# Context attentions: each product of probabilities and values in four column tiles of 32 queries in place of two of 64

## The chip, the cores and the metric

The kernel runs on one core of one Trainium2 chip. The metric is the device time of one execution in microseconds (us); for the kernel before the median of three runs is 1125.13 us (1124.1 to 1125.45). PE is the matrix engine (TensorE), PEld its weight loads, DVE, ACT and POOL are the vector, scalar and GpSimd engines, SP is the engine that issues most of the DMAs.

## The reference, cut to what matters

The reference is a four-layer chain over `x` of shape (8, 256, 256): eight samples of 256 tokens, width 256. Three of its steps are cross-attentions to a context of 77 positions per sample, with 16 heads of width 16; they differ in projections, norms and mask or bias, but all end in the same two lines (layer 0 is shown):

```python
attn = jax.nn.softmax(scores * D_QKV ** (-0.5), axis=-1)
out = jnp.einsum('bhts,bhsk->bhtk', attn, v)
```

Between and behind them stand a quantized feed-forward layer with a convolution, a self-attention with a mixture of eight experts, a routed spline layer, a pair of products with the context, and a quantized product. All of that is untouched here.

## The kernel before, in words

A context attention (`lay` 0, 1, 2) works through `NT` = 16 query tiles of `P` = 128 tokens, two for each sample; `u` is the tile. The probabilities of all 16 heads of a tile stand side by side, 16 × 77 = 1232 columns, and are cut into `NCH` = 10 chunks of 128 columns, whatever head they belong to. A chunk touches two or three heads. The values stand in `a_VB`, for each chunk a block-diagonal matrix of 128 rows and 17 columns per head touched (16 values and a column of ones, which gives the sum of the probabilities): 34 columns for five of the chunks, 51 for the other five.

For each tile the steps are, on the engines named:

- PE, `scores` (L1079): queries times keys, in four row tiles of 32 rows, 154 columns each, into PSUM banks 0 to 3.
- DVE: in layers 0 and 2 the mask or bias is added (L476) and the row maximum taken (L478), POOL subtracts it (L727); in layer 1 DVE takes the maximum (L464) and subtracts it (L467). ACT takes the exponential (L863).
- PE, `probs` (L1089): the ten chunks are transposed in three groups of 4, 4 and 2; ACT copies them from PSUM to SBUF (L868, `a_PT`) and so frees the bank.
- PE, `outputs` (L1113): for each chunk the transposed probabilities are the stationary operand and `a_VB` the moving one; the output of 128 queries is made in pieces of `OUT_COLS` queries, each in its own column tile of the array and its own partitions of PSUM bank 6 or 7. The chunks accumulate. The groups 0, 1 and 2 are three bursts, with other steps of PE between them.
- DVE: reciprocal of the sums (L485) and the product with it (L486); PE `turned` (L1120) transposes, ACT copies (L889), PE `projected` (L1126) multiplies by the output weights, DVE adds the residual (L493).

PE is fed by a program order written out by hand in `att_pe`. In the steady part of a layer it is, for tile `u`: `turned(u - 1)`, `scores(u + 2)`, `outputs(u, 0)`, `probs(u, 2)`, `outputs(u, 1)`, `projected(u - 1)`, `outputs(u, 2)`, projections and transposes for later samples (`extra`, L1003 to L1037), then `probs(u + 1, 0)` and `probs(u + 1, 1)`. `outputs` waits once per group for ACT's copy (semaphore `ring_free`), group 0 also for the residual of tile `u - 2` (`y_done`); its last product tells DVE that the tile is full (`o_full`).

All of these products are fp32. The trace holds two weight loads and two matmuls for each fp32 product of the program: 3 layers × 16 tiles × 10 chunks × 2 pieces = 960 products of L1113 stand as 1920 pairs. Where products of several tiles of the array follow each other, the pairs come in groups with one pair for every tile.

Of the kernel before, what the change touches and what calls it, by code (L numbers as in the profile page):

```python
# [123 lines left out]
def program(nc, pack0, pack1, pack2, x_in, ctx_in, ctxT_in, w1T_in, w2T_in, ew1_in, ew2_in, out):  # L124
    with ExitStack() as ctx:
# [128 lines left out]
        for c in range(NCH):  # L254
            at, done = CHUNKS[c], (CHUNKS[c - 1] + P if c else 0)
            while done < at + P:
# [1 line left out]
                end = min((h + 1) * S2, at + P)  # L258
                PIECES.append((c, h - FIRST[c], done - at, end - at, h, done - h * S2, end - h * S2))
                done = end  # L260
        QROWS, OUT_COLS = 32, 64

        KB_WORDS, VB_WORDS, V_WORDS = C * 2 * B * S2, NCH * MAXS * B * (DH + 1), H * B * (DH + 1)
        F_END = 3 * C * FF + FC * (S + 2) + FC * 3 * P
# [3337 lines left out]
```

## Time and profile before

| | |
|---|---|
| median of three runs | 1125.13 us (1124.1 to 1125.45) |
| the profiled execution's own time | 1122.43 us |
| its span, first to last instruction | 1120.7 us |
| PE busy | 1049.6 us, 94% of the span, 8906 matmuls |
| PE weight loads busy | 826.1 us, 74%, 8906 loads |
| DVE busy | 748.5 us, 67% |
| ACT busy | 469.1 us, 42% |
| POOL busy | 531.8 us, 47% |
| mean granted clock of TensorE | 0.986 |
| context attention 0 | about 33 to 137 us |
| context attention 1 | about 250 to 371 us |
| context attention 2 | about 890 to 1007 us |

A busy PE is one that has an instruction in flight; since matmuls overlap and their ends are modelled, its rate is read from the distance of starts, not from the mean duration of one. All times in the rows are microseconds from the span's start unless they are marked ns. The chain of work that ended last is followed back from an end to what released each step; a row of it gives start, length and the work, so that the lengths add up to the time.

### The profile page before, as it was taken

How to read it: one execution, taken by the hardware profiler on the slowest of the kernel's cores; microseconds unless marked ns; L12 is line 12 of the kernel's file. 1: busy time of each engine (PE TensorE's matmuls, PEld its weight loads, DVE VectorE, ACT ScalarE, POOL GpSimd, SP SyncE). 2: the span in 40 equal slices, each digit the busy share in tenths (PEclk: the TensorE clock that was granted, in tenths of full speed). 3: DMA queues.
4: the chain of work that ended last, by engine and by line, in shares of the span. 5: the costliest groups of instructions: out<-in, count | busy, mean ns of one | idle time of the engine just before them, and what ended most of it. 6: DMA issues, size and time to landing. Idle time of an engine off the chain costs nothing.

```text
span 1120.7 us, 23972 instructions
## 1 busy us (share of the span) xinstructions
PE 1049.6 (94%) x8906; PEld 826.1 (74%) x8906; DVE 748.5 (67%) x1698; ACT 469.1 (42%) x940; POOL 531.8 (47%) x526
## 2 busy tenths in 40 slices
PE   9999889988899999999989999999999999999896
PEld 5676656666676567999868999999998567765564
DVE  4899879999987448889842222222222899987794
ACT  2555677775565202121112222222222446654475
POOL 5645335577873214768764010000354757541464
PEclk9999999999999999999969999999999989999999
DMA  5999900002000300000147141311221200000001
GB/s 186 368 404 389 388 8 2 23 4 91 2 1 2 107 0 1 1 11 29 57 145 304 60 174 46 113 37 37 66 80 38 67 11 11 1 1 1 0 20 57
DMA packets 45137, 93.78 MB, mean 84 GB/s; under 512 B 3934, under 2 KB 19071, under 8 KB 42487
## 3 DMA queue, kind: packets, MB, share of 16 engines
q1 hardware_dynamic: 36646, 62.24, 15.7%
q0 software_dynamic: 7104, 29.14, 7.2%
q8 instruction: 59, 0.97, 0.3%
q10 hardware_dynamic: 1296, 1.18, 0.3%
q14 instruction: 32, 0.25, 0.1%
HBM read 39.02 MB, written 51.51 MB: 81 GB/s over the span
## 4 chain that ended last, share of the span: by engine, by line
PE 64%; DVE 19%; POOL 5%; ACT 5%; issue 4%; DMA 2%; POOLq 1%; PEldq 0%; DVEq 0%; ACTq 0%; SPq 0%; PEld 0%
PE PS L2520 11%; PE PS L2530 11%; PE PS L1113 4%; PE PS L2029 4%; PE PS L2385 3%; PE PS L1089 3%; PE PS L1126 3%; PE PS L1079 2%; PE PS L1908 2%; PE PS L2374 2%; PE PS L1743 2%; POOL big L695 2%; DVE scr L476 2%; PE PS L1037 1%; PE PS L970 1%
## 5 line engine op out<-in xcount | busy, mean ns | idle before, releaser
L2554 ACT ACTIVATE scr<-PS,W 128x128 f32<-128x128 f32 x148 | 53.5, 367 | 191.1 <-PE PS L2520 191.1
L2520 PEld LDWEIGHTS PS<-scr 128*128 128x128 f32 x992 | 116.5, 192 | 5.5 <-issue 1.8
L2520 PE MATMUL PS<-scr 128*128 128x128 f32 x992 | 118.7, 276 | 1.9 <-issue 1.5
L2530 PE MATMUL PS<-scr 128*128 128x256 f32 x496 | 112.2, 379 | 0.0
L2585 DVE TENSOR_SCALAR scr<-PS,W 128x128 f32<-128x128 f32 x148 | 51.2, 350 | 88.0 <-PE PS L2520 88.0
L727 POOL TENSOR_TENSOR scr<-scr,small 128x1232 f32<-128x1232 f32 x32 | 72.0, 2250 | 73.1 <-DVE small L478 73.0
L2591 DVE TENSOR_TENSOR scr<-PS,W 128x256 f32<-128x256 f32 x37 | 15.7, 425 | 127.0 <-PE PS L2530 123.1
L2530 PEld LDWEIGHTS PS<-scr 128*128 128x128 f32 x496 | 91.8, 190 | 11.2
L868 ACT ACTIVATE big<-PS 128x512 f32<-128x512 f32 x144 | 73.0, 523 | 58.7 <-PE PS L1089 58.1
L2631 POOL DMA_DIRECT2D expert_out<-scr x28 | 15.2, 544 | 161.4 <-DVE scr L2591 159.5
L1089 PE MATMUL PS<-W,scr 128*128 128x128 f32 x480 | 78.6, 284 | 9.4 <-ACT big L846 3.0
L1089 PEld LDWEIGHTS PS<-W,scr 128*128 128x128 f32 x480 | 52.2, 141 | 23.9 <-ACT big L846 4.6
L2385 PE MATMUL PS<-W,scr 128*128 128x128 f32 x512 | 61.1, 278 | 2.4 <-DVE scr L2140 2.4
L1113 PEld LDWEIGHTS PS<-scr,big 128*64 128x64 f32 x1280 | 45.2, 137 | 22.0 <-issue 20.5
L2385 PEld LDWEIGHTS PS<-W,scr 128*128 128x128 f32 x512 | 58.5, 192 | 3.4 <-DVE scr L2140 3.3
L863 ACT ACTIVATE scr<-scr 128x1232 f32<-128x1232 f32 x48 | 58.7, 1223 | 4.3 <-POOL scr L727 2.7
L1908 PE MATMUL PS<-identb 128*128 128x512 bf16 x225 | 58.5, 402 | 0.3 <-ACT big L868 0.3
L1113 PE MATMUL PS<-scr,big 128*64 128x34 f32 (+1 forms) x1280 | 56.7, 228 | 1.1 <-ACT big L868 0.9
L1126 PE MATMUL PS<-W,big 128*128 128x256 f32 x192 | 55.3, 410 | 0.5 <-ACT big L889 0.5
L695 POOL TENSOR_TENSOR big<-big,neghalf 128x32 f32<-128x32 f32 x8 | 45.5, 5687 | 15.9 <-DVE big L431 15.7
L1743 PE MATMUL PS<-big,W 64*64 64x256 f32 x768 | 47.0, 382 | 1.3 <-ACT scr L1662 1.3
L478 DVE TENSOR_REDUCE small<-scr 128x16 f32<-128x1232 f32 x32 | 45.9, 1436 | 1.1
(432 smaller groups left out, 2424.1 us busy)
## 6 DMA issues: line engine op xcount, KB each, us to landing
expert_in<-zeros SPq DMA_DIRECT2D x1, 19712.0 KB, 59.9
expert_out<-zeros SPq DMA_DIRECT2D x1, 19712.0 KB, 112.4
scr<-ew_in POOLq DMA_DIRECT2D x12, 1024.0 KB, 6.4
scr<-expert_in SPq DMA_DIRECT2D x38, 128.0 KB, 2.1
big<-ew_in POOLq DMA_DIRECT2D x4, 1024.0 KB, 8.5
expert_out<-scr POOLq DMA_DIRECT2D x28, 128.0 KB, 2.0
W<-pack SPq DMA_DIRECT2D x1, 2458.0 KB, 8.6
W<-pack SPq DMA_DIRECT2D x1, 2152.0 KB, 9.1
```

Of the source, the lines that this page charges most:

```text
L695: g.tensor_tensor(a_qr[j % 2], a_qvar[j % 2], neghalf[:, 0:T * H], ALU.pow).then_inc(s["qr_ready"], 1)
L727: g.tensor_tensor(sc3, sc3, a_mx[u % 3].unsqueeze(2).broadcast_to([P, H, S2]), ALU.subtract).then_inc(s["sub_ready"], 1)
L863: a.activation(a_sc[lay][u % 3], a_sc[lay][u % 3], ACT.Exp, scale=scale).then_inc(s["p_ready"], 1)
L868: a.activation(a_PT[lay][u % 2][:, 4 * g:4 * g + n, :], bank(ring_bank(lay, "p", u, g), n * P).rearrange("p (c n) -> p c n", c=n), ACT.Cop ...
L1089: ins = pe.transpose(bank(b, P, k * P), a_sc[lay][u % 3][:, at:at + P], ident)
L1113: ins = pe.matmul(PS[k:k + OUT_COLS, 6 + u % 2, at:at + n * (DH + 1)], a_PT[lay][u % 2][:, c, k:k + OUT_COLS], a_VB[lay][:, c, 0:n, u // T ...
L1126: ins = pe.matmul(bank(6 + u % 2, D, D), a_OT[lay][:, c, :], wo[:, c, :], start=(c == 0), stop=(c == C - 1))
L1743: ins = pe.matmul(PS[c * HALF:(c + 1) * HALF, conv_bank(i, p, r), 0:S], f_taps[rows, f, j, rows], f_G[rows, f, j:j + S], start=(j == 0), s ...
L1908: pe.matmul(bank(b, size, at), identb[:, :], identb[:, :].unsqueeze(1).broadcast_to([P, size // P, P]), start=True, stop=True)
L2385: ins = pe.matmul(bank(4, P, c * P), vp[:, t, c * P:(c + 1) * P], ident, start=(t == 0), stop=(t == B - 1))
L2520: ins = pe.matmul(bank(1 + f % 4, G), e_w1[slot][:, k, f * P:(f + 1) * P], e_xT[:, k, :], start=(k == 0), stop=(k == C - 1))
L2530: ins = pe.matmul(bank(5 + t, D), e_h[:, f, t * P:(t + 1) * P], e_w2[slot][:, f, :], start=(f == 0), stop=(f == FC - 1))
```

## The change

One constant: the width of the pieces in which `outputs` makes the 128 queries of a tile.

```diff
-        QROWS, OUT_COLS = 32, 64
+        QROWS, OUT_COLS = 32, 32
```

`OUT_COLS` is used in one place only:

```python
for k in range(0, P, OUT_COLS):
    ins = pe.matmul(PS[k:k + OUT_COLS, 6 + u % 2, at:at + n * (DH + 1)], a_PT[lay][u % 2][:, c, k:k + OUT_COLS],
```

So each chunk takes four products with 32 stationary columns, in the column tiles at 0, 32, 64 and 96, in place of two with 64, at 0 and 64. Each of them streams the same 34 or 51 columns as before. 960 products become 1920, and 1920 pairs of weight load and matmul become 3840. No wait, buffer, bank, order or other instruction is changed.

## Rows read from the trace of the kernel before

**Rows 1.** Busy time of each engine in the three context attentions
```profile
core 0: us, PE busy (x) PEld busy (x) DVE busy (x) ACT busy (x) POOL busy (x), PEclk, DMA share, GB/s
33.00:137.00 104.00, 95.31 (x1182) 72.53 (x1180) 95.22 (x148) 56.04 (x100) 52.41 (x46) 1.00 1.04 391
250.00:371.00 121.00, 108.23 (x1301) 81.02 (x1298) 101.02 (x193) 69.82 (x122) 77.88 (x45) 1.00 0.06 22
890.00:1007.00 117.00, 111.13 (x1276) 84.05 (x1274) 106.32 (x206) 69.72 (x131) 66.54 (x82) 0.97 0.03 8
```

**Rows 2.** Chain that ended last, by line, of the same three stretches
```profile
by line: DVE scr L423 13.7%; DVE scr L476 12.5%; PE PS L1113 9.3%; DVE small L478 8.7%; issue 8.1%; PE PS L1079 7.3%; PE PS L1089 7.1%; PE PS L1126 6.1%; PE PS L1120 4.4%; DVE big L486 3.7%; DVE big L1386 2.3%; PE PS L1037 1.9%; ACT scr L82
...
by line: PE PS L1113 11.7%; POOL big L695 9.3%; PE PS L1089 8.5%; PE PS L1034 8.3%; issue 7.9%; PE PS L1126 7.9%; PE PS L1079 6.2%; POOLq L219 5.3%; DVE small L464 4.7%; DVE scr L467 3.6%; ACT big L834 3.5%; PE PS L1120 3.1%; ACT big L841 2
...
by line: PE PS L1113 16.7%; PE PS L1089 11.2%; PE PS L1126 10.8%; PE PS L1037 7.6%; PE PS L1079 7.4%; PE PS L1014 4.7%; PE PS L1017 4.5%; issue 4.1%; DVE scr L476 3.5%; PE PS L1120 3.1%; PE PS L1003 3.1%; PE PS L1008 3.1%; ACT big L849 2.6%
```

**Rows 3.** The chain in layer 2, 938 to 941 us: start, length, work
```profile
938.28 0.60 PE PS L1113 x16
...
939.25 0.60 PE PS L1113 x16
...
940.92 0.36 PE PS L1113 x8
```

**Rows 4.** Weight loads of L1113 inside two windows: window, length, PEld busy (count)
```profile
121.09:121.11 0.02, 0.01 (x2) 1.00 1.11 410
121.09:121.51 0.42, 0.41 (x16) 1.00 1.02 380
```

**Rows 5.** Chain in the expert layer: streams of 128 (L2520) and 256 (L2530)
```profile
683.73 3.57 PE PS L2520 x32
687.52 3.46 PE PS L2530 x16
```

**Rows 6.** Matmuls of L1079 (four row tiles) inside windows: window, length, PE busy (count)
```profile
120.35:120.40 0.05, 0.04 (x4) 1.00 1.09 410
120.35:120.63 0.28, 0.27 (x8) 1.00 0.99 358
120.35:120.76 0.41, 0.40 (x12) 1.00 1.06 380
120.35:120.89 0.54, 0.53 (x16) 1.00 1.02 372
```

**Rows 7.** Groups by shape: line, engine, shape, count, busy, mean ns of one
```profile
L2520 PEld LDWEIGHTS PS<-scr 128*128 128x128 f32 x992 | 116.5, 192 | 5.5 <-issue 1.8 <-ACT scr L2554 1.3 <-DVE scr L2585 0.5
...
L1113 PEld LDWEIGHTS PS<-scr,big 128*64 128x64 f32 x1280 | 45.2, 137 | 22.0 <-issue 20.5 <-ACT big L868 1.3
```

**Rows 8.** Weight loads of L1743 inside two windows, columns as before
```profile
143.45:143.47 0.02, 0.01 (x1) 1.00 0.00 0
...
143.45:143.57 0.12, 0.11 (x8) 1.00 0.00 0
```

**Rows 9.** Chain in layer 0, where DVE sets the pace
```profile
66.16 1.45 DVE scr L476
...
67.63 1.16 DVE small L478
...
69.32 2.55 DVE scr L423 x2
...
72.07 0.42 DVE big L486
```

**Rows 10.** Who waited for whom on DVE in layer 2 (us, times, longest)
```profile
DVE X L493 <- PE PS L1126: 4.9, 4, 1.7
```

**Rows 11.** Busy time and granted clock where it falls in layer 2
```profile
908.00:912.00 4.00, 1.87 (x21) 1.47 (x22) 3.93 (x6) 2.44 (x5) 2.51 (x3) 0.91 0.00 0
912.00:916.00 4.00, 4.00 (x48) 2.93 (x42) 3.90 (x8) 1.33 (x3) 0.99 (x3) 0.50 0.00 0
916.00:920.00 4.00, 4.00 (x25) 2.91 (x22) 2.30 (x8) 0.77 (x1) 3.10 (x2) 0.74 0.00 0
```

## What the change should do to the time

> **What bounds the kernel now.** I read three views, in this order. First the busy times of the stretches in which L1113 runs [rows 1]: in attention 0 PE is busy 95.3 of 104 us and DVE 95.2, in attention 1 it is 108.2 and 101.0 of 121, in attention 2 111.1 and 106.3 of 117. Both engines are nearly full everywhere, so a step taken from one of them is paid back only until the other is late. Then the chain of each stretch by line [rows 2]: L1113 holds 9.3% of 104 us, 11.7% of 121 and 16.7% of 117, that is 9.7, 14.2 and 19.5 us, together 43.4 us. In attention 0 the head of the list is DVE (L423, L476, L478), in attention 2 it is PE alone. Then one tile of the chain in attention 2 [rows 3]: the three bursts of L1113 take 0.60, 0.60 and 0.36 us from their start to that of the next step, 1.56 us a tile and 74.9 us for 48 tiles. So 43.4 / 74.9 = 58% of what L1113 takes lies on the path.
>
> **What paces a burst.** Two loads start in the window that ends at 121.11 us, one for each column tile, and sixteen by 121.51 [rows 4]: seven further groups of two in 0.40 us, 57 to 58 ns a group. A group here is one load and one matmul in each tile. Which of the two sets the 58 ns? Loads of 128 columns before streams of 128 go at 3.57 us / 32 = 112 ns, streams of 256 at 3.46 / 16 = 216 ns [rows 5]. In L1079 a group of four row tiles that stream 154 columns takes 0.13 us [rows 6]. Two streams give (216 - 131) / 102 = 0.83 ns a column, so 51 columns should take 131 - 103 × 0.83 = 45 ns and 34 columns 31 ns. Both are below 58: the burst waits for its weight loads. 128 columns at 112 ns and 64 at 58 make 0.84 ns a column; the mean durations, 192 and 137 ns [rows 7], differ by as much. The loads of the tiles overlap each other, or four of 128 columns could not fit into the 0.13 us of [rows 6].
>
> **The change part by part.** Removed: half the columns of each load. A load of 32 columns should be ready after 58 - 27 = 31 ns. The streams keep 34 and 51 columns, now in four tiles at once. If all four work beside each other, as the four row tiles of [rows 6] do, a group takes 31 ns where it streams 34 columns (load and stream alike) and 45 ns where it streams 51 (the stream is the bound). There are ten groups of each kind in a tile (five chunks of each kind, two pairs per product and column tile): 10 × 27 + 10 × 13 = 400 ns saved.
>
> Added: 1920 pairs, 40 a tile. That four pairs follow each other closely is in [rows 6]: four matmuls within 0.04 us of the window, so some 7 to 10 ns each. The last of four tiles then ends about 14 ns later than the last of two, three times a tile: 42 ns given back, and on the way of `o_full`, for which DVE's L485 waits. Net 0.36 us a tile, 23% of 1.56, or 17 us of PE's time in all.
>
> No wait is added. The changes of tiling between L1113 and its neighbours stay six a tile, so I cost them at nothing; they lie in PE's own time, and nothing hides them if they grow. The longer instruction stream (23972 records become 27812) I cost at nothing too, since PE handles a tile's pairs in some 6 us now, 70 ns or more for each, and would have half as many again. The copies, banks and semaphores are the same.
>
> What reaches the end: 23% of the on-path 43.4 us is 10.0 us, 2.2, 3.3 and 4.5 by attention. That is the ceiling, since time off the chain returns nothing. What is late next takes part of it. In attention 0 it is DVE, which runs from L476 through L478 and L423 to L486 with hardly a gap [rows 9] and has only 9 us idle: 1.3 us remain. In attention 1 DVE has 20 us idle, but ACT's and POOL's steps on the chain (L834, L841, L695) need not move: 2.4. In attention 2 PE falls to 111.1 - 5.8 = 105.3 us, just below DVE's 106.3; DVE waits there 4.9 us for L1126 [rows 10], which comes earlier now: 3.7. Sum 7.4 us. The profiled execution would go from 1122.4 to 1115.0 (span 1120.7 to 1113.3). It lies 2.7 us below the median of the runs shown, which I shift alike: 1125.1 - 7.4 = 1117.7.
>
> **Bounds of what the trace doesn't show.** No row has four column tiles, a load of 32 columns, or eight instructions in 31 ns. The cost of a group lies between 31 ns (load and stream as above) and 4 × 27 = 108 ns, if the 27 ns for each pair, which is the closest that pairs follow over a whole burst ([rows 4]: 16 loads in 0.40 us), were a limit of issue and not of the load. I take 31 and 45 because the nearest row, four tiles in L1079, has four starts within 0.04 us. [Rows 8] say a little more: after an idle PE eight loads of four tiles have started within 0.11 us, and these too are held up by 64-column loads.
>
> **A rule that speaks against it.** [Rows 6] show four matmuls of different tiles that start within 0.04 us. The Trainium skill's "TensorEngine Tiling (Array Packing)", section Instruction Overhead, gives each matmul some 60 cycles whatever it streams and advises against taking the tiling factor from a dimension that is already small. At 2.4 GHz that is an estimate of 25 ns a pair, 100 ns a group, and by it the kernel gets slower. No row here shows such a limit across tiles. The Trainium skill's "TensorE: Matmul & The Clock Gate", section Part 3, has about 4 ns for each further tile, and by that the sum above stands.
>
> **The rivals.**
> Slower, by a limit of issue: each pair costs 27 ns of PE's queue, in whatever tile. A group then takes 108 ns in place of 58, 20 groups 1.0 us, with the ends 1.04 us a tile and 50 us in all. 58% of it is 29 us; since PE would then be the bound in all three attentions, up to all 50. I take 39: 1164. It decides from 14 ns a pair on, where four make 56 ns and the ends the rest. For it: no burst of the trace is closer than 27 ns a pair. Against it: [rows 6], and that 27 is just what 64-column loads make.
> No change, by a milder limit of issue: at 14 ns a pair, the rate of the eight loads of [rows 8], a group takes 56 ns, 20 × 2 - 42 = 0: 1125. At 10 ns a pair it would be 1120. For it: that is as much as the trace proves. Against it: those loads had another reason.
> The change doesn't do what it says: four column tiles load only two by two. A group takes 2 × 31 = 62 ns, 0.12 us a tile more, 5.9 us in all, 58% of it 3.4: 1128.5. For it: no row has more than two column tiles at work. Against: the loads of four row tiles overlap.
> The clock: in attention 2 the granted clock falls to half once (0.91, 0.50 and 0.74 in three windows of 4 us make some 6.8 us at 1.2 GHz in place of 2.4), behind a stretch in which PE was busy 1.87 of 4 us [rows 11]. PE gets 0.36 us more of idle a tile wherever DVE sets the pace. One more fall takes up to 3.4 us of my gain back, 1121; without this one the gain is so much larger, 1114.
>
> **How the numbers follow.** Forecast 0.60, the milder limit 0.16, two by two 0.06, the hard limit 0.13, the clock 0.05. The likeliest gives 1117.7. Its own range is 1114 (nearly the whole ceiling) to 1122 (a third of it). The range given, 1113.5 to 1129, takes in the mild limit, two by two and the clock, and leaves out the hard limit and little else. About 0.2% or 2.3 us is what a measurement of this kernel can tell from no change. Faster by more: 0.63, nearly all of the forecast and some of the mild limit and the clock. Within it: 0.17. Slower: 0.20, from the hard limit, two by two and late surprises.
>
> **What would show each step.** L1113 with 3840 loads whose mean is near 137 - 27 = 110 ns. 32 loads of a burst within about 0.30 us in place of 16 in 0.41; a burst of 0.45 to 0.47 us in the chain in place of 0.60, and 0.29 in place of 0.36. L1113's busy time down by some 17 us. L1113's share of the chain lowest in attention 0, DVE's share up in all three, most of the gain in attention 2. The prediction is wrong if a group takes over 56 ns, if groups hold fewer than four pairs, or if the changes of tiling grow; its size is wrong if DVE's chain was as long as PE's all along.

## The result, and the profile after

| | before | after |
|---|---|---|
| median (20 runs each) | 1124.58 us (1122.65 to 1128.52) | 1127.51 us (1124.65 to 1131.69) |
| ratio, 95% interval | | 1.0024 [1.0013, 1.0034] |
| profiled execution, own time | 1122.43 us | 1128.8 us |
| its span | 1120.7 us | 1126.9 us |
| mean granted clock of TensorE | 0.986 | 0.981 |
| attention 0, first L1079 to last L1126 | 115.2 us | 121.5 us |
| attention 1, the same | 120.6 us | 119.4 us |
| attention 2, the same | 130.0 us | 129.2 us |

Medians, ratios and intervals in this document are of executions in the usual state; one execution of a kernel of experiment 4 (1708.73 us at a granted clock of 0.555) is left out of its numbers.

The kernel got slower by 0.24%; 7.4 us of gain were forecast. The lengths of the attentions are those of the profiled executions, from the start of the first L1079 to the start of the last L1126. In the profiled execution the time is lost mainly in one place: attention 0 is 6.3 us longer, the two others are 1.2 and 0.8 us shorter. (Outside of them the stretch between attentions 1 and 2 is some 3 us longer in the profiled execution; the next section but one comes back to it.)

The page of after: busy time and records, the instruction queue of PE (packets, MB, share), the chain by engine, and the two groups of L1113 (count, then busy, mean ns of one, idle before):

```profile
span 1126.9 us, 27812 instructions
PE 1038.3 (92%) x10826; PEld 811.5 (72%) x10826; DVE 748.8 (66%) x1698; ACT 469.3 (42%) x940; POOL 532.1 (47%) x526
...
q8 instruction: 74, 1.21, 0.4%
...
PE 58%; DVE 25%; issue 6%; ACT 4%; POOL 4%; DMA 2%; POOLq 1%; PEldq 0%; DVEq 0%; another core or an unknown queue 0%; SPq 0%; ACTq 0%; PEld 0%
...
L1113 PEld LDWEIGHTS PS<-scr,big 128*32 128x32 f32 x2560 | 33.2, 111 | 27.8 <-issue 26.1
...
L1113 PE MATMUL PS<-scr,big 128*32 128x51 f32 (+1 forms) x2560 | 46.3, 207 | 5.9 <-issue 4.8
```

The loads fell from a mean of 137 to 111 ns [rows 7], and L1113 keeps PE busy for 69.1 us in place of 85.8. PE as a whole is busy 11 us less, and the span is 6.2 us longer. L1113 is idle before its loads for 26.1 us to "issue", before 20.5 [rows 7]: time in which PE waited for nothing that the profile shows.

The three attentions after, the answer to [rows 1] (window, length, PE, PEld, DVE, ACT, POOL busy, granted clock, DMA share, GB/s); the windows are longer where the stretch is:

```profile
33.00:143.00 110.00, 92.81 (x1773) 68.65 (x1760) 94.39 (x148) 56.28 (x104) 51.76 (x45) 0.97 1.01 380
255.00:375.00 120.00, 103.99 (x1943) 75.90 (x1941) 100.22 (x192) 70.22 (x122) 78.21 (x45) 0.99 0.06 23
897.00:1013.00 116.00, 105.64 (x1915) 77.09 (x1914) 108.38 (x205) 69.94 (x131) 66.08 (x81) 0.99 0.03 8
```

In attention 0 PE is busy 2.5 us less and DVE as long as before, in six us more: neither engine's work explains the added time. The same stretches in the chain by line:

```profile
by line: issue 12.1%; DVE scr L423 9.8%; DVE scr L476 9.2%; PE PS L1113 9.2%; PE PS L1079 9.0%; PE PS L1089 8.6%; PE PS L1126 8.0%; DVE small L478 5.4%; PE PS L1120 4.4%; PE PS L1037 3.5%; DVE big L486 3.1%; DVE X L493 2.7%; DVE big L1386 2
...
by line: issue 9.7%; POOL big L695 9.4%; PE PS L1034 9.2%; DVE small L464 7.2%; PE PS L1113 6.9%; PE PS L1079 6.3%; PE PS L1089 6.3%; PE PS L1126 6.2%; POOLq L219 5.3%; DVE scr L467 4.3%; PE PS L1120 3.4%; ACT big L834 2.9%; ACT big L841 2.
...
by line: DVE scr L476 14.4%; issue 12.1%; DVE scr L2674 7.4%; DVE small L478 6.7%; DVE big L486 5.2%; PE PS L1079 5.0%; DVE scr L2689 4.7%; DVE X L493 3.9%; DVE W L504 3.3%; DVE small L410 2.6%; DVE small L2678 2.6%; PE PS L1113 2.4%; DVE s
```

Against [rows 2], "issue" heads the list in attention 0 with 12.1% in place of 8.1%. DVE's three lines of it (L423, L476, L478) fall from 34.9% together to 24.4%. In attention 1 L1113 goes from 11.7% to 6.9%. In attention 2 the list was nearly PE alone; now DVE heads it and L1113 is down from 16.7% to 2.4%.

**The burst itself is as forecast.** The weight loads of PE in attention 0, 120.6 to 122.7 us (start, length, work), where two bursts and their neighbours stand:

```profile
120.64 0.41 PEld L1113 LDWEIGHTS PS<-scr,big 128*32 128x32 f32 x32 [0.16 <-issue]
121.12 0.20 PEld L1089 LDWEIGHTS PS<-W,scr 128*128 128x128 f32 x2
121.49 0.40 PEld L1113 LDWEIGHTS PS<-scr,big 128*32 128x32 f32 x32 [0.17 <-issue]
121.96 0.73 PEld L1126 LDWEIGHTS PS<-W,big 128*128 128x128 f32 x4
```

The 32 loads of a burst all start within 0.30 us (the 0.41 us of the line runs on to the end of the last one), where 16 took 0.41 us to start [rows 4]. The next step starts after 0.48 and 0.47 us; in [rows 3] it was 0.60. The starts of single loads in the trace come in fours, 7 ns apart. The next group of four follows most often 30 ns (28 to 37) behind one that streams 34 columns, and 44 or 45 ns behind one that streams 51. With the third burst of 16 pairs (0.26 us) a tile's L1113 takes 1.21 us where it took 1.56.

**What is new is PE running dry inside a burst,** that is, starting no further instruction though the program has no wait there. The same view of after at 45.5 to 50 us:

```profile
45.49 0.18 PEld L1113 LDWEIGHTS PS<-scr,big 128*32 128x32 f32 x8
45.74 0.73 PEld L1126 LDWEIGHTS PS<-W,big 128*128 128x128 f32 x4
46.81 0.14 PEld L1113 LDWEIGHTS PS<-scr,big 128*32 128x32 f32 x5 [0.33 <-issue]
49.39 0.21 PEld L1113 LDWEIGHTS PS<-scr,big 128*32 128x32 f32 x11 [2.44 <-issue]
49.64 0.31 PEld L1003 LDWEIGHTS PS<-W,scr 128*128 128x128 f32 x3
```

The third burst of a tile, 16 pairs, stops after five loads and goes on 2.4 us later. Between its fifth and its sixth load the program has no wait; the only wait of a burst is ahead of its first product. At that moment a packet stands in the queue that brings PE's own instructions. DMA queues in 46.85 to 46.95 us (packets, MB, share):

```profile
q1 hardware_dynamic: 16, 0.03, 84.0%
q8 instruction: 1, 0.02, 55.1%
```

The packet starts at 46.90, just behind the last start on PE (46.87), ends at 47.79, and PE resumes at 49.39. The trace of after has seven such stops in attention 0, with their last start at 38.1, 46.9, 64.4, 83.2, 112.7, 126.7 and 134.6 us, in L1126, L1113, L1089 and L1079; PE has neither a load nor a matmul in flight in them for 0.8, 2.3, 2.4, 0.4, 0.9, 1.2 and 0.4 us, 8.4 in all. Each ends 1.3 to 1.6 us behind the end of such a packet. The trace of before has none: there the longest idle of these lines that is put down to "issue" is 0.4 us. The waits of PE's loads in 20 to 137 us, of after and then of before (us in total, times, longest):

```profile
PEld PS L1113 <- issue: 15.8, 49, 2.4
...
PEld PS L1089 <- issue: 3.4, 3, 2.6
...
PEld PS L1126 <- issue: 1.2, 1, 1.2
```
```profile
PEld PS L1113 <- issue: 10.3, 46, 0.4
...
PEld PS L1089 <- issue: 0.7, 2, 0.4
```

So the first theory was: **PE's instructions come by DMA, in blocks; with 40 pairs more a tile they are used up faster, and while the two large fills of `expert_in` and `expert_out` (19.7 MB each, L3401, issued by SP at 28 to 30 us) keep the DMA engines full, the next block comes late.** The page counts 59 packets of 16 KB in that queue before:

```profile
q8 instruction: 59, 0.97, 0.3%
```

and 74 after. 15 × 16384 bytes for 3840 records more make 64 bytes each, 256 records a block. (The kernels of the experiments fit this within one packet: 10 or 11 for 2560 records more, 6 for 1280.) The DMA queues in 33 to 137 us, before and then after:

```profile
q1 hardware_dynamic: 19691, 40.53, 103.8%
q8 instruction: 9, 0.15, 0.5%
```
```profile
q1 hardware_dynamic: 19555, 40.65, 103.5%
q8 instruction: 13, 0.21, 0.7%
```

The rival theories: four column tiles are themselves what stalls (a limit of the array or the issue); the granted clock, which falls twice in attention 0 of after and not at all in that of before, is the cause of the lost time and not its consequence; or the longer stream costs wherever it runs, fills or none.

### The profile page after: what moved, and what is told of

Read it like the earlier page. It is cut to its first block, busy times and chain, and to the rows that moved or that the text cites. A ratio compares the mean times of both kernels' runs of the same rounds, so it can differ in the third digit from the quotient of the medians.

```text
span 1126.9 us, 27812 instructions
## 1 busy us (share of the span) xinstructions
PE 1038.3 (92%) x10826; PEld 811.5 (72%) x10826; DVE 748.8 (66%) x1698; ACT 469.3 (42%) x940; POOL 532.1 (47%) x526
## 3 DMA queue, kind: packets, MB, share of 16 engines
q8 instruction: 74, 1.21, 0.4%
## 4 chain that ended last, share of the span: by engine, by line
PE 58%; DVE 25%; issue 6%; ACT 4%; POOL 4%; DMA 2%; POOLq 1%; PEldq 0%; DVEq 0%; another core or an unknown queue 0%; SPq 0%; ACTq 0%; PEld 0%
PE PS L2520 11%; PE PS L2530 11%; PE PS L2029 4%; PE PS L2385 4%; DVE scr L476 2%; PE PS L1908 2%; PE PS L1079 2%; PE PS L1113 2%; PE PS L2374 2%; PE PS L1089 2%; PE PS L1126 2%; PE PS L1743 2%; POOL big L695 2%; DVE small L478 1%; PE PS L2411 1%
## 5 line engine op out<-in xcount | busy, mean ns | idle before, releaser
L2520 PEld LDWEIGHTS PS<-scr 128*128 128x128 f32 x992 | 116.5, 192 | 5.5 <-issue 1.8
L2520 PE MATMUL PS<-scr 128*128 128x128 f32 x992 | 118.7, 276 | 1.9 <-issue 1.6
L2530 PE MATMUL PS<-scr 128*128 128x256 f32 x496 | 112.2, 379 | 0.0
L2530 PEld LDWEIGHTS PS<-scr 128*128 128x128 f32 x496 | 91.8, 190 | 11.2
L1089 PE MATMUL PS<-W,scr 128*128 128x128 f32 x480 | 78.8, 285 | 11.5 <-ACT big L846 3.0
L1089 PEld LDWEIGHTS PS<-W,scr 128*128 128x128 f32 x480 | 52.7, 142 | 26.5 <-ACT big L846 4.6
L2385 PE MATMUL PS<-W,scr 128*128 128x128 f32 x512 | 61.7, 279 | 2.4 <-DVE scr L2140 2.4
L2385 PEld LDWEIGHTS PS<-W,scr 128*128 128x128 f32 x512 | 59.2, 194 | 3.5 <-DVE scr L2140 3.3
L1126 PE MATMUL PS<-W,big 128*128 128x256 f32 x192 | 54.6, 405 | 1.3 <-issue 0.8
L1113 PEld LDWEIGHTS PS<-scr,big 128*32 128x32 f32 x2560 | 33.2, 111 | 27.8 <-issue 26.1
L695 POOL TENSOR_TENSOR big<-big,neghalf 128x32 f32<-128x32 f32 x8 | 45.5, 5688 | 15.0 <-DVE big L431 14.8
L1113 PE MATMUL PS<-scr,big 128*32 128x51 f32 (+1 forms) x2560 | 46.3, 207 | 5.9 <-issue 4.8
L1743 PE MATMUL PS<-big,W 64*64 64x256 f32 x768 | 47.0, 382 | 1.3 <-ACT scr L1662 1.3
L478 DVE TENSOR_REDUCE small<-scr 128x16 f32<-128x1232 f32 x32 | 46.0, 1436 | 1.1
```

What stands on the lines that cost most here:

```text
L695: g.tensor_tensor(a_qr[j % 2], a_qvar[j % 2], neghalf[:, 0:T * H], ALU.pow).then_inc(s["qr_ready"], 1)
L1089: ins = pe.transpose(bank(b, P, k * P), a_sc[lay][u % 3][:, at:at + P], ident)
L1113: ins = pe.matmul(PS[k:k + OUT_COLS, 6 + u % 2, at:at + n * (DH + 1)], a_PT[lay][u % 2][:, c, k:k + OUT_COLS], a_VB[lay][:, c, 0:n, u // T ...
L1126: ins = pe.matmul(bank(6 + u % 2, D, D), a_OT[lay][:, c, :], wo[:, c, :], start=(c == 0), stop=(c == C - 1))
L1743: ins = pe.matmul(PS[c * HALF:(c + 1) * HALF, conv_bank(i, p, r), 0:S], f_taps[rows, f, j, rows], f_G[rows, f, j:j + S], start=(j == 0), s ...
L2385: ins = pe.matmul(bank(4, P, c * P), vp[:, t, c * P:(c + 1) * P], ident, start=(t == 0), stop=(t == B - 1))
```

## The experiments

`OUT_COLS` by attention was made a table: `OUT_COLS = {0: w0, 1: w1, 2: w2}`, used as `OUT_COLS[lay]` in L1112 and L1113. "64/32/32" below is its three widths. A ratio is to the kernel before on the same chip, with its 95% interval.

**1. Each attention by itself.**

```diff
-        QROWS, OUT_COLS = 32, 64
+        QROWS, OUT_COLS = 32, {0: 64, 1: 32, 2: 32}
```

> Attention 0 keeps two column tiles of 64; attentions 1 and 2 have four of 32. Theory A (the loss is made in attention 0, where PE's instruction stream is used up faster than its blocks arrive while two zero fills keep the DMA engines full): attention 0 is back at 115 us, no stall in it, the other two keep their 1.3 and 0.9 us; in all 1 to 3 us faster than the kernel before, 0.997 to 0.999. Theory B (the loss lies in the clock, which falls wherever PE has more idle time): attentions 1 and 2 still show extra falls, and the kernel is 0 to 2 us slower than before. Theory C (the longer stream costs time in all places): slower by 1 us or more.

```diff
-        QROWS, OUT_COLS = 32, 64
+        QROWS, OUT_COLS = 32, {0: 32, 1: 64, 2: 64}
```

> Attention 0 has four column tiles of 32, the other two keep two of 64: the other half of the change. Theory A: nearly all of the loss and more is here, attention 0 takes about 120 us in place of 115 with four to seven stalls of 0.4 to 2.5 us, each ending about 1.45 us behind the end of an instruction fetch; in all 4 to 6 us slower, 1.003 to 1.006. Theories B and C: 1 to 2 us slower, a third to a half of what the whole change costs more, with no such stalls.

64/32/32: 1119.99 us, ratio 0.9965 [0.9951, 0.998]. 32/64/64: 1128.80 us, 1.0041 [1.0015, 1.0066]. The loss is in attention 0 alone (122.1 us long in the second kernel, with eight stops, each 1.2 to 1.6 us behind a block's end); where only attentions 1 and 2 are narrow the kernel is faster than before. In the first kernel attention 0 takes 116.7 us and not 115, without a stop: the granted clock falls there once, at 127.2 us, though the work is that of before. It has one stop, at the head of attention 1, and there the DMA engines are busy as well (weight loads in 265 to 269 us, and the DMA share, next to last number, of 262 to 270):

```profile
266.14 0.90 PEld L1089 LDWEIGHTS PS<-W,scr 128*128 128x128 f32 x7
268.56 0.14 PEld L1089 LDWEIGHTS PS<-W,scr 128*128 128x128 f32 x1 [1.52 <-issue]
```
```profile
262.00:270.00 8.00, 6.08 (x159) 4.41 (x163) 7.83 (x16) 4.73 (x9) 7.92 (x4) 1.00 0.70 284
```

**2. The fills behind the attention.** One wait ahead of the two fills keeps them back until attention 0 has written its last tile:

```diff
             sp.wait_ge(consts_ready, 2)
+            sp.wait_ge(at_["y_done"], NT)
             for table in (xg_dram, yg_dram):
```

once with 64 and once with 32 in all attentions.

> The kernel before with the two zero fills issued only when attention 0 has ended. It is the reference for the next run. Theory A: attention 0 had no stalls before, so it stays near 115 us or gains at most 1 us; the fills then run beside the feed-forward layer and end near 250 us, in the beginning of attention 1, whose values may come late by some us. In all 0.998 to 1.005. Theories B and C say the same.

> The changed kernel with the two zero fills issued only when attention 0 has ended, to be compared with the run before this one. Theory A: with the DMA engines free the blocks of the instruction stream arrive in time, attention 0 has no stall over 0.3 us and becomes shorter than with tiles of 64, by 1 to 2 us; 3 to 5 us in all faster than the run before. Theory B: the falls of the clock in attention 0 stay without the stalls and the gain is under 1 us. Theory C: attention 0 stays at 119 us or more.

Late fills and 64: 1122.94 us, 0.9997 [0.9974, 1.0019]. Late fills and 32: 1117.40 us, 0.9950 [0.9931, 0.9969]. Attention 0 is 115.2 us long with 64, as with early fills, and 115.1 with 32 in place of 121.5. The width costs 0.24% with early fills and gains about 0.47% with late ones, 5.5 us by the two medians. The expectation had attention 0 1 to 2 us shorter with 32 than with 64, and no stop over 0.3 us; in this execution it is 0.1 us shorter, with one fall of the clock and one stop. A second execution of the kernel, in experiment 7, takes 113.6 us. The waits of the loads in 20 to 137 us, and the DMA queues in 33 to 137, late fills and 32:

```profile
PEld PS L1113 <- issue: 10.8, 47, 0.7
```
```profile
q1 hardware_dynamic: 231, 1.14, 3.6%
q8 instruction: 14, 0.23, 0.9%
```

As many blocks, the same four column tiles, no other traffic, and the idle put down to "issue" is back at 10.8 us with a longest of 0.7 (one stop, at 37.9 us, where other loads are still under way). That rules out the tiling as the cause of the stops, and the longer stream by itself. The blocks show what the fills do: the packets take no longer beside them (0.88 to 1.1 us in attention 0, against 0.88 to 1.5 without), but the shortest distance between two blocks of after is 6.5 us and from 81 us on it is 6.9 to 8.1, while without fills blocks follow at 4.7 and 5.0 us where PE uses them up so fast (at 3.7 in the second execution). So a block starts late; it doesn't run slowly.

**3. One fill early.** 32 everywhere, `expert_out`'s fill behind the attention:

```diff
             for table in (xg_dram, yg_dram):
+                if table is yg_dram:
+                    sp.wait_ge(at_["y_done"], NT)
```

> The changed kernel (32 in all three attentions) with the first zero fill where it was and the second issued when attention 0 has ended, so that the DMA engines are full for only the first half of attention 0, until about 80 us. Theory A: the stalls at 38, 47 and 64 us stay, those at 83, 113, 127 and 135 us vanish; attention 0 takes 118 to 119 us, between 121.5 and 115.0. If the stalls came from the longer stream alone, all stay; if from another cause of the place in the kernel, they stay where they were.

1124.16 us, 1.0012 [0.9995, 1.0028]. Where the stops are follows the fill. The DMA share (next to last number) in three stretches of attention 0:

```profile
22.00:80.00 58.00, 0.94 1.00 362
80.00:100.00 20.00, 1.00 0.37 139
100.00:137.00 37.00, 0.95 0.01 2
```

The stops at 38.7, 47.5, 64.8 and 83.7 us are there, the last just before the fill ends (the expectation had that one gone); the three of after behind 100 us are gone. The idle of L1113 put down to "issue" behind 91 us is 5.1 us with a longest of 0.7, in after 7.9 with 1.3. The size was missed: attention 0 was to take 118 to 119 us and took 120.9. The first L1126 behind tile 12 starts at 126.4 us, 2.1 earlier than in after, and then 2.1 us are lost in tiles 13 and 14, where the granted clock falls at 133 us. (A tile's time here and below runs from its first L1126 to that of the next.) The kernel has a further stop, 271.7 to 274.0 us, in attention 1, though its second fill has landed at 198.7 us. The DMA engines are again busy there, with a share of 0.61 in 270 to 275 us.

**4. A longer stream without the change.** Width 64, but 80 small products in each tile of attention 0 before the first burst; their results are used by nothing. Once with early and once with late fills. They are 160 records a tile, twice what the change adds (3840 in 48 tiles are 80 a tile; the expectation has them as equal), so the effect is to be larger than that of the change.

```diff
                 pe.wait_ge(s["ring_free"], ring[(lay, "p", u, g)] + 1)
+                if lay == 0 and g == 0:
+                    for q in range(80):
+                        k = q % 4 * 32
+                        pe.matmul(PS[k:k + 32, 6 + u % 2, 504:508], identb[:, k:k + 32], identb[:, 0:4], start=True, stop=True,
+                                  skip_group_check=True)
```

> Tiles of 64 everywhere, zero fills where they were. In attention 0 only, each query tile issues 80 further small bf16 products (32 stationary columns, 4 streamed, over the four column tiles, results unused) ahead of its first product of probabilities and values: 160 more instructions on PE for a tile, as many as the change adds, but with L1113 as before. Cost on PE some 0.6 to 1 us a tile. Theory A (the length of the instruction stream while the DMA engines are full makes the stalls): attention 0 shows 4 to 8 stalls of 0.4 to 2.5 us that end some 1.4 us behind the end of an instruction fetch, and takes 5 us or more over the next run. If the stalls belonged to column tiles of 32, there are none.

> The run before with both zero fills issued when attention 0 has ended: its reference. Theory A: at most one stall in attention 0 (the one near 38 us, when the first loads still run); the price of the added instructions alone, 0 to 6 us over 115 us, since DVE sets the pace there.

Early fills: 1162.94 us, 1.0346 [1.032, 1.0373]; attention 0 takes 147.5 us. Late fills: 1138.45 us (three executions, 1132.49 to 1143.28), 1.0091 [1.0056, 1.0125]; 126.3 us. Beside the 115.2 us of before, the same added instructions cost attention 0 32 us with early fills and 11 us with late ones, so the fills' part is 21 us of it; by the two medians it is 24 us, from few and scattered executions. (The two profiled ones, 1154.60 and 1143.28 us, are only 11 apart, since that with late fills has more falls of the clock in attentions 1 and 2.) The waits of the loads in 20 to 137 us, early fills and then late (L1118 here is L1113 of before):

```profile
PEld PS L1118 <- issue: 16.6, 28, 2.8
```
```profile
PEld PS L1118 <- issue: 7.3, 28, 0.7
```

and one of the seven stops with early fills:

```profile
124.62 0.25 PEld L1118 LDWEIGHTS PS<-scr,big 128*64 128x64 f32 x5 [0.33 <-issue]
127.67 0.29 PEld L1118 LDWEIGHTS PS<-scr,big 128*64 128x64 f32 x3 [2.80 <-issue]
```

Here products with 64 columns stop in the same manner, 1.4 us behind the end of a block. The stops make up 11.0 us, with late fills 1.4 (one stop, at 37 us), which is less than the 21 us between the two kernels. The rest goes with the clock, which is at half for 34 us of attention 0 with early fills and for 7 with late ones. The late-fills kernel missed its expectation (0 to 6 us in attention 0) by 5: from the start of the first to the end of the last, a tile's small products take PE 0.77 us, in all 14 us with the stop, in a stretch that PE is nearly full in. These two kernels vary length and fills. They do not vary the tiling of L1113, but the small products lie in four column tiles themselves; that tiling has no part is shown by experiment 2.

**5. Early or late with 64 in attention 0.**

Late fills, 64/32/32:

> Both zero fills issued when attention 0 has ended, tiles of 64 in attention 0, of 32 in the other two. Against the kernel with late fills and 32 everywhere (1117.4 us, 0.995 of before) it tells what tiles of 32 give in attention 0 once the stalls are gone. By the stretches of the traces (115.0 with 32, 115.2 with 64) it is the same within 1 us, 0.995 to 0.997 of before; by the forecast of 1.3 us for attention 0 it is 1.3 us slower.

1119.06 us, 0.9963 [0.9946, 0.9981]. Beside it early fills and 64/32/32 gave 0.9965: for a stream of the old length the place of the fills makes no difference, as between before and late fills with 64. Beside 0.9950 and 0.9965 for 32 everywhere with late fills, the whole-kernel times can't tell the two widths in attention 0 apart; the stretches can, below.

**6. Is DVE next late?** In attentions 1 and 2 the row maximum is taken over 38 of the 77 keys (L464, L478), which makes DVE's step shorter. With 64 everywhere, and with 64/32/32.

```diff
-                    ch.link(v.tensor_reduce(mx.rearrange("p (m r w) -> p r m w", m=C, w=2), ps, AX.X, ALU.max))
+                    ch.link(v.tensor_reduce(mx.rearrange("p (m r w) -> p r m w", m=C, w=2), ps[:, :, :, :, 0:HALF_KEYS], AX.X, ALU.max))
```

> Tiles of 64 in all three attentions, and in attentions 1 and 2 DVE's row maximum is taken over 38 of a head's 77 keys (what is computed is changed in this: another shift than the row maximum is subtracted before the exponential). DVE's work falls by some 0.7 us a tile, 22 us in all. It is the reference for the next run. If DVE set the pace of both attentions, they become 5 to 10 us shorter in all; if PE did, 0 to 3 us.

> As the run before, with tiles of 32 in attentions 1 and 2 (64 in attention 0), again with the maximum over 38 of 77 keys in these two. If DVE is what took the rest of PE's gain (the two attentions gave 2 to 3 us of the 11 us that PE saves there), the gap between the two runs grows to 6 us or more. If it stays at 2 to 4 us, something else is next late: ACT, or the order of the steps on PE itself.

1117.62 us, 0.9952 [0.9934, 0.997], and 1108.82 us, 0.9882 [0.9861, 0.9903]. With a lighter DVE the width in attentions 1 and 2 is worth 8.8 us by the medians; with DVE as it is, 2.9 (64/32/32 against before, experiment 1). By stretch it is 4.9 us in attention 1 (121.3 to 116.4) and 2.6 in attention 2 (125.0 to 122.4); part of the 4.9 is the clock, which is at half for 6.8 us there with 64 and for 3.4 with 32. In attention 2 neither has a fall. This agrees with [rows 1] and with the chain of after: much of what the width doesn't return in attention 2 is held by DVE. For attention 1 the two clocks leave it open how much.

**7. The clock.** Late fills, 32 everywhere, and eight products in place of three that keep PE at work behind the first tile of attention 1:

```diff
-                        clocked(pe, 7, 3)
+                        clocked(pe, 7, 8)
```

> Late fills, tiles of 32 everywhere, and eight in place of three filler matmuls behind the first tile of attention 1, just ahead of the idle time in which the granted clock fell at 272 us. If that fall is what took 1.3 us of attention 1's gain, its second tile takes about 12 us in place of 13.1 and the kernel is 1 us faster than the next run. If the fillers fall into PE's busy time or the clock falls all the same, no change or up to 1 us slower.

> The same kernel as e4, on the chip and with the runs of the kernel before of this call, as the reference of the run before and to see how firm 0.995 is: 0.993 to 0.997.

1120.37 us, 0.9954 [0.9938, 0.9969], and without the edit, in the same call, 1120.97, 0.9965 [0.9947, 0.9983]. The tile behind the edit took 9.7 us in place of 13.0, but what lies ahead of it, from the first L1079 to the first L1126, takes 19.4 us in place of 16.8, with the added products and a stop of the kind above at 265.7 us in it; the two ratios can't be told apart. The second kernel is the one of experiment 2 again, and it confirms that it is faster than before, by 0.2 to 0.5% here and 0.3 to 0.7% there.

**What the granted clock does in attention 0.** Around the two long stops of after (window, length, busy times, then the granted clock):

```profile
44.00:48.00 4.00, 3.07 (x91) 2.10 (x87) 3.37 (x4) 1.97 (x4) 0.55 (x2) 1.00 1.05 405
48.00:52.00 4.00, 2.35 (x24) 2.08 (x25) 2.58 (x9) 1.08 (x2) 3.73 (x4) 0.87 1.05 403
52.00:56.00 4.00, 4.00 (x88) 2.97 (x87) 2.02 (x2) 1.90 (x4) 0.00 (x0) 0.70 1.05 403
...
64.00:68.00 4.00, 1.57 (x27) 1.39 (x13) 3.56 (x9) 0.83 (x2) 3.29 (x3) 1.00 1.05 404
68.00:72.00 4.00, 4.00 (x87) 2.84 (x86) 1.97 (x2) 1.82 (x5) 0.85 (x2) 0.57 1.05 408
```

PE is dry at 46.9 and at 64.4 us, and at 51.0 and 68.1 the clock goes to half (1.2 GHz) for 3.4 us each. Each fall begins after its stop has ended, so the stop isn't its consequence; but the time lost grows by it. Tiles 2 and 4 of after, in which this falls, take 9.6 and 9.1 us in place of 6.1 and 6.2: 6.4 us together, with 4.7 us of stops in them, and as much as the whole attention is longer. What the later stops cost, 0.7 to 1.1 us in tiles 6, 10 and 12, is returned in other tiles. Late fills and 32 (experiment 2) had three falls in attentions 0 and 1, at 125.5, 272.2 and 350.7 us, and has the lowest ratio of the kernels with DVE as it is: falls alone don't make after slow.

## Why the prediction was wrong, point by point

**The pace of a burst: right.** A group at about 30 ns with 34 columns and 45 with 51, forecast 31 and 45; 32 loads started within 0.30 us, as forecast; loads with a mean of 111 ns, forecast 110; bursts of 0.47 to 0.48 and 0.26 us, forecast 0.45 to 0.47 and 0.29; L1113 16.7 us less of PE, forecast 17. Bounding the unknown by four row tiles of L1079 [rows 6] and not by the closest pairs of a burst [rows 4] was the right choice. Both issue limits fall, since a group of four in 30 ns leaves at most 8 ns for a pair. Column tiles two by two fall as well. The rule of the Trainium skill's "TensorEngine Tiling (Array Packing)", section Instruction Overhead, some 60 cycles for each matmul, would make a group of four 100 ns, an estimate at 2.4 GHz; measured are 30 and 45, so the trace doesn't agree with it across tiles of the array.

**"The longer instruction stream … I cost at nothing": this step failed.** The reason given was that PE handles a tile's pairs in 6 us, 70 ns or more for each, and would have half as many again. That looks at the rate at which PE can issue, and never at where the instructions come from. The page of before has the row: a queue of its own, 59 packets, beside a DMA share of 1.04 in attention 0 [rows 1]. A cost of nothing needs the name of what hides it, and the prediction named none for the fetches. What hid them was that PE used up a block in some 12 us (9 packets in 104 us) and now in 8 (13 packets). Its price was 8.4 us of idle PE, a further 6.8 us at half clock, and 6.3 us of time in attention 0, where 1.3 were to be gained: 7.6 of the 13.6 us between the span that was forecast (1113.3) and the span of after (1126.9). Attention 1 is 1.2 us short of its forecast gain, attention 2 2.9, and the stretch between them is 2.9 longer; ahead of attention 0 and behind attention 2 1.0 us is returned. (The profiled execution of after lies 1.3 us above its median, that of before 2.2 below: by medians the change costs 2.9 us, not 6.2.) Nowhere did the prediction have a rival for it; its rivals for a slower kernel all sat in the array. So the array's work was sized rightly, and the kernel is slower by a term put at nothing.

**Attention 0: mechanism right once the cover is there.** With no clock fall, and no stop but the one near 38 us, 64 takes 115.2 (before, and experiment 2) and 32 takes 113.6 us (late fills, experiment 7); with one fall at 125 to 127 us, 64 takes 116.7 and 116.8 (experiments 1 and 5) and 32 115.1 and 115.0 (late fills, experiments 2 and 7). So the width is worth 1.6 to 1.7 us, forecast 1.3; these are single executions. With DVE as next late this was read well from [rows 1, 9]: tiles 2 to 9 take the same time at both widths.

**Attention 1: right.** With no clock fall in it 64 takes 120.6 us and 32 takes 118.0 (64/32/32, early fills, its stop included): 2.6, forecast 2.4. With one fall it is 122.1 (32/64/64) against 118.9 and 119.3 (late fills, experiment 7) and 119.4 (after); with two, 32 takes 119.9 to 120.4.

**Attention 2: over-sized.** Forecast 3.7. With a fall of 6.8 us in it 64 takes 130.0 us and 32 takes 129.2 to 129.7: 0.3 to 0.8. With one of 3.4 us 64 takes 128.6 (late fills) and 32 takes 129.2 (after): 0.6 longer. Only 32/64/64, whose fall comes later, at 932 us, takes 131.6. The 4.9 us in which DVE waited for L1126 [rows 10] were taken as time that a faster PE returns. But PE at 105.3 of 117 us and DVE at 106.3 were level, and not every tile was one of PE's. Tiles 5 and 7 got 0.4 us shorter, tiles 9 and 11 got longer, from 9.7 to 10.2 and 10.3 us. The chain through tile 9, before and then after:

```profile
by line: PE PS L1037 15.9%; PE PS L1113 14.2%; PE PS L1089 12.8%; ACT scr L863 11.1%; PE PS L1126 9.6%; PE PS L1017 9.5%; PE PS L1014 9.2%; PE PS L1079 6.7%; ACT big L849 5.5%; PE PS L1008 5.3%; issue 2.4%; PE PS L1120 2.0%; ACT big L868 1.
```
```profile
by line: DVE scr L476 26.4%; issue 18.2%; DVE scr L2689 10.3%; DVE small L410 6.9%; DVE W L504 6.1%; DVE small L3025 5.7%; DVE W L3030 5.3%; DVE X L2694 4.8%; DVE big L486 3.9%; DVE X L493 3.8%; DVE small L2681 2.3%; DVE small L413 2.0%; DV
```

It was nearly all PE and is nearly all DVE, with work in DVE's order (L2689, L3025, L3030) that the prediction never weighed. "Its size is wrong if DVE's chain was as long as PE's all along": experiment 6 points to that in attention 2, where with a lighter DVE, and no fall of the clock, the width does return 2.6 us. Why those two tiles are longer by half a microsecond is open.

**The clock: half right, in the wrong place.** A rival had one more fall, at a price of up to 3.4 us, for idle that DVE leaves to PE. Two falls came, behind stops that it had not foreseen. Without the stops (late fills and 32) attentions 0 and 1 together have one fall in one execution and three in the other, before none; a fall late in attention 0 costs 1.5 us. That these falls come from the width isn't shown: 64/32/32 has one in attention 0 too, where its width is 64.

**The range** reached to 1129 for two-by-two tiles and the mild limit; that 1127.5 is inside it is luck, since it got there for another reason. Of the signs named, most of the gain was to be in attention 2 and L1113's share of the chain lowest in attention 0; it is 9.2% in attention 0 and 2.4% in attention 2.

**What is left open.** Why a block isn't asked for earlier, or waits, beside the fills: the trace shows its packet, not its request. Why only some of the 13 blocks are late: in after none from 81 us on follows the last by less than 7.0 us, where late fills and 32 have 4.7 to 6.0 for every second one. And the 2.9 us between attentions 1 and 2 (155.7 us from the first L2385 to the first L2520, before 152.8), where the code isn't changed. Another kernel of the same widths, late fills and 32, took 151.8 us for that stretch in one execution and 155.5 in the other, the longer one with an extra fall of the clock at 550 us as after has one at 560; so these traces don't show that it belongs to the change.

## What to carry to other kernels

When an edit multiplies the instructions of an engine, look at the instruction queue of the page and at the DMA share of the stretch: how long does one block last there, and are the DMA engines free to bring the next? More and smaller instructions were cheap in the array here (7 ns a pair) and dear beside a bulk transfer, and then it is the transfer that should move: 32 everywhere with the fills behind attention 0 is 0.35 to 0.5% faster than before (1117.4 and 1121.0 us against 1122.9 and 1125.5 on the same chips), where the edit alone was 0.24% slower. And where two engines are level, take a faster one as worth the difference between them, not the other's waits for it.

## What the runs showed of the hardware

- PE's instructions come in blocks of 16 KB through a DMA queue of their own, 256 records of 64 bytes each; a block's packet takes 0.9 to 1.7 us. Beside DMA engines with a share of about 1.04 blocks follow at 5.8 us or more (32/64/64; 6.5 in after), and those of the two longest stops of after start only when PE has started its last instruction; with late fills the same stream has them at 3.7 to 4.7 us, that of experiment 4 at 3.6. Work resumes 1.2 to 1.6 us behind the packet's end. The profile shows such a stop as "issue", in the middle of a burst, with no releaser.
- Pairs of load and matmul in four column tiles start 7 ns apart. fp32 loads of 64 and 128 columns pace at 58 and 112 ns. Groups with loads of 32 go at about 30 ns where they stream 34 columns, which doesn't tell load from stream, and at 45 where they stream 51: there the stream is the bound, as the load was at 58.
- Around each stop of PE of over 2 us in the kernel after and in 32/64/64, the granted clock goes to half for 3.4 or 6.8 us: in after it falls at 51.0 and 68.1 us for stops from 46.9 and 64.4. The stop of 2.1 us at 271.7 us of experiment 3 is followed by no fall until 290.1 us.
